# State-space block moved from one software stream to the other, with the loop over batches cut inside the scan

## The chip, the cores and the metric

The kernel runs on one core of a Trainium2 chip. The time is device microseconds from launch to end, the median of several executions. The engines are TensorE (PE), VectorE (DVE), ScalarE (ACT) and GpSimd (POOL); SyncE (SP) only issues DMAs. Each engine works through its own instruction list in order, and waits on semaphores that other engines raise.

## The reference, cut to what matters

Sixteen batches of 512 tokens by 128 channels go through four blocks; batches do not depend on each other.

1. Selective scan, in two directions: after a norm, `delta = softplus(...)`, and for each of 16 states per direction `h[t] = exp(delta*A)[t] * h[t-1] + (delta*B*x)[t]` along the 512 tokens, `y += C*h`. That is 32 scans of 128 x 512 per batch. A feed-forward with a router multiplies the result by a gate.
2. Head of the state-space block: norm, a query projection with rotation, a second norm, and the step sizes `dt` (softplus of 16 numbers per partition, and their running sum `acs`).
3. State-space block in chunks of 128 tokens (`Y_diag` and `Y_off` with decay matrices `exp(segsum)`, a 4-tap convolution, SiLU, a gated norm, output projection).
4. Two transformer layers with local attention (8 heads of 64, windows of 64 tokens), each followed by layer norm and a GELU feed-forward; then the result is multiplied with the state-space result and added to the residual.

```
h = x + o @ wo ;  h = shift_token(h)       # lower 64 channels shifted by one token
```

`shift_token` is why each layer's input lies in a tile `xs0` of 513 columns: channels 0 to 63 at column t, channels 64 to 127 at column t+1.

## The kernel before, in words

A batch's work is written as two streams of numbered slots. Each engine has a generator per part (`prologue`, `scan`, `head`, `stage_b`), and `both` (called from `run`) interleaves them into one instruction list per engine: for each slot of stream B its instructions, then all slots of stream A up to `pace(slot + 1) - 1`. The order is thus fixed by hand through the table `PACE` (pairs of a B slot and an A slot, linear between them).

- Stream A for batch i: `scan(i)`, one slot per state (32), then `A_END` and `head(i)` (8 slots), then `prologue(i+1)` (9 slots: transpose, norm, projections, router feed-forward, `delta`, `u`, the gate).
- Stream B for batch i-1, `stage_b`: 11 slots of the state-space block ("mamba" below), then per layer 15 slots of attention (`UNITS_END`: projections in slots 0 to 3, head-major copies in 2 to 5, eight score units in 4 to 11, their transposes 2 slots and their value products 3 slots later) and 5 slots of output projection, norm and feed-forward; two slots for the final product.

One step of the loop is A of batch i beside B of batch i-1. Before the loop, prologue, scan and head of batch 0 and the prologue of batch 1 run alone (the fill); after it, B of the last batch runs alone (the drain). The last step has no prologue.

A state of the scan takes: PE two selection matmuls `B{k}` and `C{k}` (L505) into PSUM; DVE `bx = u * B` (L1149) from PSUM to SBUF; ACT `dA = exp(...)` (L858) and the copy `Cs` (L864); DVE the scan `hst` (L1157) on `dA` and `bx`; POOL `hc = hst * Cs` (L1392); PE the accumulation of `hc` into bank 2 (L493).

PSUM banks are handed out in rings. Ring A holds banks 0 and 1, ring B banks 3 to 6; banks 2 and 7 are accumulators. A job takes the next bank of its ring and PE waits until the job that had it before was read. `A_JOBS` and `B_JOBS` name each job with the semaphore that tells that it was read. So `B{k}` and `C{k}` alternate between the two banks of ring A, and `B{k}`'s bank is free when `bx` is written:

```
+ [job for k in range(2 * NS) for job in ((f"B{k}", "a_bx", k + 1), (f"C{k}", "a_Cs", k + 1))]
PACE = [(0, 2), (LAYER, 16), (LAYER + UNITS_END, 28), (LAYER + LAYER_SLOTS, HEAD), (LAYER + LAYER_SLOTS + 5, PRO),
        (LAYER + LAYER_SLOTS + UNITS_END, A_SLOTS - 1), (B_END, A_SLOTS - 1), (B_SLOTS, A_SLOTS)]
```

With `LAYER = 11` that puts two states ahead of B's first slot, fourteen more beside the state-space block, twelve beside the attention of layer 0, the head beside the first five slots of layer 1, the prologue beside the rest of its attention, and nothing but the last slot beside the second feed-forward.

The input of a layer is made by one DVE addition over 128 channels (`xa` L1331, `yB` L1351) and two ACT copies of 64 channels each into `xs0` (`shifted`, L784 and L785). ACT holds one set of function tables; `tables()` (L779) loads the set with Exp and Ln, and SiLU or GELU bring a load of their own.

Of the kernel before, what the change touches and what calls it, by code (L numbers as in the profile page):

```python
# [23 lines left out]
P = 128  # L24
# [10 lines left out]
NL = 2  # L35
# [16 lines left out]
def offsets(widths):  # L52
    at, out = 0, {}
    for name, n in widths:
# [16 lines left out]
B_JOBS = ([("ab0", "m_ld", 1)] + [(f"ab{q}", "m_ea", q) for q in range(1, NT)]  # L71
# [3 lines left out]
          + [("y0", "m_y2", 1), ("y1", "m_y2", 2), ("yss", "m_yln", 1), ("mo", "m_sm1", 1)])  # L75
NW = T // WIN
UNITS = [(half, g) for half in range(2) for g in range(HA // 2)]
# [4 lines left out]
for _l in range(NL):  # L82
# [11 lines left out]
    B_JOBS += [(f"wo{_l}", "f_xa", _l + 1), (f"lmean{_l}", "f_xr", _l + 1), (f"lvar{_l}", "f_ln", _l + 1)]  # L94
    for _m in range(3):
        B_JOBS += [(f"fg{_l}{_m}", "f_gl", 3 * _l + _m + 1), (f"fa{_l}{_m}", "f_ha", 3 * _l + _m + 1)]
    B_JOBS += [(f"fd{_l}", "f_y", _l + 1)]


SCAN = 0  # L100
A_END = SCAN + 2 * NS
HEAD = A_END + 1
PRO = HEAD + 8
A_SLOTS = PRO + 9
LAYER = 11
# [4 lines left out]
PACE = [(0, 2), (LAYER, 16), (LAYER + UNITS_END, 28), (LAYER + LAYER_SLOTS, HEAD), (LAYER + LAYER_SLOTS + 5, PRO),  # L110
        (LAYER + LAYER_SLOTS + UNITS_END, A_SLOTS - 1), (B_END, A_SLOTS - 1), (B_SLOTS, A_SLOTS)]


def pace(slot):
    for (b0, a0), (b1, a1) in zip(PACE, PACE[1:]):
        if b0 <= slot <= b1:
# [6 lines left out]
           m_ysq=2, t_xs=2 * NL, f_xs=2 * NL, t_v=7 * NL, t_k=4 * NL, t_r=4 * NL, t_rln=4 * NL, t_clip=4 * NL, t_oT=4 * NL,  # L123
# [4 lines left out]
for _s in ("f_xa", "f_xc", "f_sq", "f_ln", "f_r", "f_xr", "f_hn", "f_y"):  # L128
    PER[_s] = NL


def build(nc, x, wpack, cpack, mask, tables, taps, rowpack, out):
    ctx = ExitStack()
    with ctx:
# [27 lines left out]
        rings = {"A": (banks[0:2], A_JOBS), "B": (banks[3:7], B_JOBS)}  # L162
# [100 lines left out]
        sm = sb("sm", [T])  # L263
        tmp1 = sb("tmp1", [2, T])
# [20 lines left out]
        xsA, x2, xo = xs0, x1b, xa  # L285
        gl, ha = on, kT
        big1 = kT[:, :, :].rearrange("p q (h l) -> p q h l", h=HM)
        big2 = oT[:, :, :].rearrange("p q (h l) -> p q h l", h=HM)
        xbc, sz, y3 = vt[:, 0:4], vt[:, 4:6], PT
        xdt = xdt_b[:, :, :].rearrange("p a (b h d) -> p (a b) h d", b=2, h=HM)  # L290
        xdd = xdd_b[:, :, :].rearrange("p a (b h d) -> p (a b) h d", b=2, h=HM)
        btok = Pm[:, 0, :].rearrange("p (q n) -> p q n", q=NT)
        onf = on[:, :, :].rearrange("p a b -> p (a b)")
# [52 lines left out]
        def run(e, prologue, scan, head, stage_b, finish):  # L346
# [3 lines left out]
            both(chain(scan(2), head(2), prologue(3)), stage_b(1, 0))  # L350
            with e.Fori(3, NB - 1) as i:
                both(chain(scan(i), head(i), prologue(e.snap(i + 1))), stage_b(e.snap(i - 1), e.snap(i - 2)))
            both(chain(scan(NB - 1), head(NB - 1)), stage_b(NB - 2, NB - 3))
            alone(stage_b(NB - 1, NB - 2))
            finish(NB - 1)
# [5 lines left out]
        def _(sp):  # L361
# [17 lines left out]
            def scan(i):  # L379
                yield A_END  # L380

            def head(i):
                yield HEAD

            def stage_b(i, ended):
                yield 2
                if ended is not None:
                    finish(ended)
# [6 lines left out]
            run(sp, prologue, scan, head, stage_b, finish)  # L395
# [4 lines left out]
        def _(pe):  # L400
# [86 lines left out]
            def scan(i):  # L487
# [7 lines left out]

                yield SCAN
                pe.wait_ge(*step("a_parts", i))
                for k in range(2 * NS):
                    yield SCAN + k
# [9 lines left out]
                yield A_END  # L509
                accumulate(2 * NS - 2)  # L510
                accumulate(2 * NS - 1)
# [45 lines left out]
            def stage_b(i, ended):  # L557
                for q in range(NT):
                    yield q // 2
                    if q == 0:  # L560
                        pe.wait_ge(*step("m_acs", i))
                    if used("B", f"ab{q}", i):
                        pe.wait_ge(*vacant("B", f"ab{q}", i))
                    b = bank("B", f"ab{q}")
# [4 lines left out]
                    last.then_inc(full("B", f"ab{q}"), 1)  # L569
                pe.wait_ge(*step("m_h", i))  # L570
                for t in range(4):
                    yield 2 + t
                    if t == 0 and ended is not None:
                        finish(ended)
                    if used("B", f"cx{t}", i):
                        pe.wait_ge(*vacant("B", f"cx{t}", i))
                    b = bank("B", f"cx{t}")
# [3 lines left out]
                    last.then_inc(full("B", f"cx{t}"), 1)  # L581
                for t in range(2):
                    norm_sum("B", f"mz{t}", i, wz_f[:, t * P:(t + 1) * P], hpad[:, 3:3 + T])
                yield 6
                pe.wait_ge(*step("m_xs", i))
                if used("B", "G", i):
                    pe.wait_ge(*vacant("B", "G", i))
                b = bank("B", "G")
                for q in range(NT):
                    ts = slice(q * P, (q + 1) * P)  # L590
                    last = mm(b[:, ts], xbc[:, 2, ts], xbc[:, 3, ts], start=True, stop=True)
                last.then_inc(full("B", "G"), 1)

                for job, t in (("bt", 2), ("xt0", 0), ("xt1", 1)):
                    if job == "xt0":
                        yield 7
                    if used("B", job, i):
                        pe.wait_ge(*vacant("B", job, i))
                    b = bank("B", job)
# [998 lines left out]
```

## Time and profile before

| | |
|---|---|
| median of 3 runs | 4658.02 us (4657.6 to 4661.66) |
| the profiled execution's own time | 4646.64 us |
| its span, first to last instruction | 4644.8 us |
| mean granted TensorE clock | 0.881 of full speed |
| PE busy | 3574.7 us (77% of the span) |
| DVE busy | 2898.1 us (62%) |
| ACT busy | 2356.1 us (51%) |
| POOL busy | 1755.3 us (38%) |
| DMA | mean 4 GB/s over the span |

The sum of all the engines' work is far from filling the span on any one of them, and the shares are averages over stretches with different limits. Matmuls overlap in their pipeline, so PE's busy time is the union of them and not a sum of single durations.

### The profile page before, as it was taken

How to read it: one execution, taken by the hardware profiler on the slowest of the kernel's cores; microseconds unless marked ns; L12 is line 12 of the kernel's file. 1: busy time of each engine (PE TensorE's matmuls, PEld its weight loads, DVE VectorE, ACT ScalarE, POOL GpSimd, SP SyncE). 2: the span in 40 equal slices, each digit the busy share in tenths (PEclk: the TensorE clock that was granted, in tenths of full speed). 3: DMA queues.
4: the chain of work that ended last, by engine and by line, in shares of the span. 5: the costliest groups of instructions: out<-in, count | busy, mean ns of one | idle time of the engine just before them, and what ended most of it. 6: DMA issues, size and time to landing. Idle time of an engine off the chain costs nothing. (4 is left out here: it accounts for less than half of the span.)

```text
span 4644.8 us, 53531 instructions
## 1 busy us (share of the span) xinstructions
PE 3574.7 (77%) x16160; PEld 1947.4 (42%) x16160; DVE 2898.1 (62%) x4687; ACT 2356.1 (51%) x4102; POOL 1755.3 (38%) x1428
## 2 busy tenths in 40 slices
PE   5777777878777777777777787778787877778776
PEld 1244344444444444344443444444344444444443
DVE  6575665757657575665756657566574765757544
ACT  3455555555555555455555555555554554545444
POOL 2253442525325253342534415244252532525332
PEclk9798889989989898888988988899898888979888
DMA  1000000000000000000000000000000000000000
GB/s 74 3 1 1 5 1 5 1 1 5 1 6 1 1 5 1 6 1 6 1 1 6 1 6 1 1 6 1 6 1 1 6 1 6 1 1 3 1 3 3
DMA packets 18378, 20.44 MB, mean 4 GB/s; under 512 B 768, under 2 KB 17152, under 8 KB 17792
## 3 DMA queue, kind: packets, MB, share of 16 engines
q1 hardware_dynamic: 18048, 16.44, 1.1%
q8 instruction: 159, 2.61, 0.2%
q14 instruction: 171, 1.40, 0.1%
HBM read 12.24 MB, written 4.19 MB: 4 GB/s over the span
## 5 line engine op out<-in xcount | busy, mean ns | idle before, releaser
L1392 POOL TENSOR_TENSOR hc<-hst,Cs 128x512 f32<-128x512 f32 x512 | 649.9, 1269 | 1735.9 <-DVE hst L1157 1721.2
L1157 DVE TENSOR_TENSOR_SCAN hst<-dA,bx 128x512 f32<-128x512 f32 x512 | 752.2, 1469 | 313.9 <-issue 164.6
L493 PE MATMUL bank<-hc,C 128*128 128x512 f32 x1024 | 581.8, 652 | 6.9 <-POOL hc L1392 6.9
L517 PE MATMUL bank<-W,xs 128*128 128x512 f32 x960 | 471.4, 628 | 39.0 <-DVE tmp L1298 33.7
L505 PE MATMUL bank<-parts,sel 96*128 96x512 bf16 x1024 | 355.9, 421 | 183.7 <-DVE bx L1149 128.7
L1468 POOL TENSOR_TENSOR Pm<-Pm,rinv 128x512 f32<-128x512 f32 x256 | 273.6, 1069 | 523.3 <-DVE rinv L1314 510.1
L1149 DVE TENSOR_TENSOR bx<-u,bank 128x512 f32<-128x512 f32 x512 | 345.5, 675 | 199.4 <-PE bank L505 170.2
L1453 POOL TENSOR_TENSOR oT<-tmp 128x512 f32<-128x512 f32 x256 | 324.5, 1268 | 273.5 <-DVE tmp L1298 181.8
L864 ACT COPY Cs<-bank 128x512 f32<-128x512 f32 x512 | 294.3, 575 | 244.2 <-PE bank L505 224.1
L983 ACT ACTIVATE Pm<-Pm 128x512 f32<-128x512 f32 x256 | 161.4, 630 | 462.6 <-DVE Pm L1323 462.6
L858 ACT ACTIVATE dA<-delta,neg_a 128x512 f32<-128x512 f32 x512 | 367.9, 719 | 44.1 <-DVE hst L1157 39.2
L683 PEld LDWEIGHTS bank<-kT,qbd 128*128 128x128 f32 x2048 | 313.4, 219 | 50.2 <-issue 37.5
L517 PEld LDWEIGHTS bank<-W,xs 128*128 128x128 f32 x960 | 190.4, 205 | 330.0 <-issue 216.2
L1461 POOL TENSOR_TENSOR oT<-oT,rqk 128x512 f32<-128x512 f32 x256 | 289.9, 1132 | 72.8 <-ACT rqk L961 58.2
L693 PE MATMUL bank<-C,Pm 128*128 128x128 f32 x1024 | 174.7, 297 | 176.9 <-POOL Pm L1468 176.8
L683 PE MATMUL bank<-kT,qbd 128*128 128x128 f32 x2048 | 310.1, 301 | 0.0
L666 PE MATMUL bank<-C,oT 128*128 128x128 f32 x1024 | 179.4, 319 | 116.1 <-DVE tmp L1298 116.0
L751 PE MATMUL bank<-tmp,W 128*128 128x512 f32 (+1 forms) x384 | 213.5, 715 | 69.2 <-DVE tmp L1338 69.2
L493 PEld LDWEIGHTS bank<-hc,C 128*128 128x128 f32 x1024 | 211.4, 210 | 110.1 <-POOL hc L1392 35.2
L505 PEld LDWEIGHTS bank<-parts,sel 96*128 96x128 bf16 x1024 | 91.8, 102 | 393.2 <-DVE bx L1149 199.2
L1293 DVE TENSOR_TENSOR tmp<-bank,rot 128x512 f32<-128x512 f32 x256 | 174.1, 680 | 106.6 <-ACT Pm L952 105.1
L579 PE MATMUL bank<-hpad,wc_f 128*128 128x512 f32 x512 | 229.8, 592 | 0.0
(226 smaller groups left out, 6322.8 us busy)
## 6 DMA issues: line engine op xcount, KB each, us to landing
W<-wpack SPq DMA_DIRECT2D x1, 4498.0 KB, 13.6
x_tok<-x SPq DMA_DIRECT2D x16, 256.0 KB, 2.9
out<-xa SPq DMA_DIRECT2D x16, 256.0 KB, 2.2
rot<-tables SPq DMA_DIRECT2D x2, 512.0 KB, 16.3
wc_f<-taps SPq DMA_DIRECT2D x1, 1024.0 KB, 19.7
C<-cpack SPq DMA_DIRECT2D x1, 721.0 KB, 14.9
Pm<-mask SPq DMA_DIRECT2D x1, 320.0 KB, 15.2
tmp<-rowpack SPq DMA_DIRECT2D x1, 256.0 KB, 17.4
```

The lines of the kernel that those rows point to most:

```text
L493: mm(y_acc[:, :], ident, hc[:, k % 2, :], start=(k == 0), stop=(k == 2 * NS - 1))\
L505: mm(b[:, :], sel16[0:96, o + s:o + s + 1].to_broadcast([96, P]), parts[0:96, d, :], start=True, stop=True)\
L517: mm(b[:, :], weights, rhs, start=True, stop=True).then_inc(full(ring, job), 1)
L683: last = mm(b[:, wi * P:(wi + 1) * P], qbd[:, g, at, :], kT[:, g, lo:lo + P], start=False, stop=(wi == 3), skip_group_check=True)
L858: f(dA[:, k % 2, :], delta[:, k // NS, :], ACT.Exp, scale=neg_a[:, k:k + 1])\
L864: nc.scalar.copy(Cs[:, k % 2, :], b[:, :]).then_inc(sem("a_Cs"), 1)
L1149: v.tensor_tensor(bx[:, k % 2, :], u[:, d, :], b[:, :], ALU.mult).then_inc(sem("a_bx"), 1)
L1157: v.tensor_tensor_scan(o, a, b, 0.0, ALU.mult, ALU.add).then_inc(sem("a_h"), 1)
L1392: g_.tensor_tensor(hc[:, k % 2, :], hst[:, k % 2, :], Cs[:, k % 2, :], ALU.mult)\
L1453: g_.tensor_tensor(qtok[:, 2 * kind + s % 2, :], tmp1[:, kind, :], tmp2[:, kind, :], ALU.add)\
L1461: g_.tensor_tensor(tok, tok, over(rqk[:, s, kind, :], DH), ALU.mult).then_inc(sem("t_qk"), 1)
L1468: g_.tensor_tensor(windows, windows, over(rinv[:, k % 2, :], P), ALU.mult).then_inc(sem("t_P"), 1)
```

## The change

The state-space block becomes a function `mamba` of its own in stream A, between `head` and the next `prologue`. Stream B keeps the two layers and the final product. The loop is cut inside the scan: a step runs the states 12 to 31 of batch i, its head, its state-space block, the prologue of batch i+1 and the states 0 to 11 of batch i+1, beside B of batch i-1.

```
+CUT = 12
 SCAN = 0
-A_END = SCAN + 2 * NS
+A_END = SCAN + 2 * NS - CUT
 HEAD = A_END + 1
-PRO = HEAD + 8
-A_SLOTS = PRO + 9
-LAYER = 11
+MAMBA = HEAD + 8
+PRO = MAMBA + 11
+SCAN1 = PRO + 9
+A_SLOTS = SCAN1 + CUT
+LAYER = 1
-PACE = [(0, 2), (LAYER, 16), (LAYER + UNITS_END, 28), ...
+PACE = [(0, 0), (LAYER, 2), (LAYER + UNITS_END, HEAD + 5), (LAYER + LAYER_SLOTS, MAMBA + 5),
+        (LAYER + LAYER_SLOTS + 7, PRO), (LAYER + LAYER_SLOTS + UNITS_END, SCAN1), (B_SLOTS, A_SLOTS)]
...
+def scan_slot(k):
+    return SCAN1 + k if k < CUT else SCAN + k - CUT
...
+            def ready(i):
+                return chain(prologue(i), scan(i, 0, CUT)) if CUT else prologue(i)
+            def body(i):
+                return chain(scan(i, CUT, 2 * NS), head(i), mamba(i))
-            alone(chain(prologue(0), scan(0), head(0), prologue(1)))
-            both(chain(scan(1), head(1), prologue(2)), stage_b(0, None))
+            alone(chain(ready(0), body(0), ready(1)))
+            both(chain(body(1), ready(2)), stage_b(0, None))
...
+                both(chain(body(i), ready(e.snap(i + 1))), stage_b(e.snap(i - 1), e.snap(i - 2)))
+            both(body(NB - 1), stage_b(NB - 2, NB - 3))
             alone(stage_b(NB - 1, NB - 2))
```

The rings change: bank 3 goes from B to A, so each has three banks. The state-space block's 21 jobs move to ring A, and its tiles now lie in tiles of the scan and the prologue (`hst`, `hc`, `bx`, `gate`, `delta`, `u`, `dA`, `Cs`, `dlow`, `xc`) that are free between a batch's last state and the next prologue. The scan multiplies `B` in place, in PSUM, and reads it there; its bank is free when the scan has ended.

```
-          + [job for k in range(2 * NS) for job in ((f"B{k}", "a_bx", k + 1), (f"C{k}", "a_Cs", k + 1))]
+          + [job for k in range(2 * NS) for job in ((f"B{k}", "a_h", k + 1), (f"C{k}", "a_Cs", k + 1))]
-        rings = {"A": (banks[0:2], A_JOBS), "B": (banks[3:7], B_JOBS)}
+        rings = {"A": (banks[0:2] + banks[3:4], A_JOBS), "B": (banks[4:7], B_JOBS)}
...
-                    v.tensor_tensor(bx[:, k % 2, :], u[:, d, :], b[:, :], ALU.mult).then_inc(sem("a_bx"), 1)
+                    v.tensor_tensor(b[:, :], u[:, d, :], b[:, :], ALU.mult).then_inc(sem("a_bx"), 1)
-                    o, a, b = hst[:, k % 2, :], dA[:, k % 2, :], bx[:, k % 2, :]
+                    o, a, b = hst[:, k % 2, :], dA[:, k % 2, :], b[:, :]
```

DVE now writes the layers' sums straight into `xs0`, in two halves of 64 channels; of ACT's copies into `xs0` only the pair ahead of layer 0 stays. ACT loads the Exp and Ln tables once more, behind the last SiLU of stream B. Inside the block DVE makes the four products with `G` ahead of `xdt`. ACT's copy `x1b` and the output of the batch before move to slots 2 to 4 of layer 0.

```
+HALVES = [(slice(0, 64), 0), (slice(64, P), 1)]
-                    v.tensor_tensor(xa[:, :], xin[:, :], b[:, :], ALU.add).then_inc(sem("f_xa"), 1)
+                    for r, o in HALVES:
+                        v.tensor_tensor(xs0[r, o:o + T], xs0[r, o:o + T], b[r, :], ALU.add).then_inc(sem("f_xs"), 1)
-                    shifted(xsA, xa, "f_xs", "f_xa", i, l + 1)
...
-                    v.scalar_tensor_tensor(out=yB[:, :], in0=b[:, :], scalar=w(f"fb2_{l}"), in1=xa[:, :],
-                                           op0=ALU.add, op1=ALU.add).then_inc(sem("f_y"), 1)
+                    for r, o in HALVES:
+                        dst = xs0[r, o:o + T] if l + 1 < NL else yB[r, :]
+                        v.scalar_tensor_tensor(out=dst, in0=b[r, :], scalar=w(f"fb2_{l}", rows=r), in1=xs0[r, o:o + T],
+                                               op0=ALU.add, op1=ALU.add).then_inc(sem("f_y"), 1)
-                        shifted(xs0, yB, "t_xs", "f_y", i, l + 1)
...
                 f(tmp2[:, 0, :], yB[:, :], ACT.Silu).then_inc(sem("g2"), 1)
+                tables()
...
+                dve.wait_ge(*step("m_G", i))
+                for q in range(NT):
+                    dve.wait_ge(*step("m_L", i, q + 1))
+                    v.tensor_tensor(big2[q], big2[q], each(G[:, q, :], HM), ALU.mult).then_inc(sem("m_M"), 1)
                 for g in range(2):
```

## Rows read from the trace of the kernel before

**Rows 1.** Page, part 1: busy time (share of the span) and instructions of each engine.

```profile
span 4644.8 us, 53531 instructions
...
PE 3574.7 (77%) x16160; PEld 1947.4 (42%) x16160; DVE 2898.1 (62%) x4687; ACT 2356.1 (51%) x4102; POOL 1755.3 (38%) x1428
```

**Rows 2.** Windows, whole steps: stretch, length, PE, PEld, DVE, ACT, POOL busy, clock, DMA.

```profile
208.50:490.50 282.00, 222.17 (x1006) 122.12 (x1006) 179.05 (x292) 146.06 (x256) 110.34 (x89) 0.88 0.00 1
490.50:768.00 277.50, 217.68 (x1010) 121.55 (x1010) 179.96 (x292) 146.34 (x257) 109.42 (x89) 0.91 0.01 3
...
3889.00:4173.50 284.50, 222.81 (x1011) 122.65 (x1011) 179.25 (x291) 145.58 (x255) 110.39 (x89) 0.88 0.01 3
4173.50:4435.80 262.30, 207.05 (x984) 116.30 (x985) 165.02 (x264) 131.00 (x233) 107.13 (x88) 0.88 0.01 2
```

**Rows 3.** Windows, one step: state-space, attention 0, feed-forward 0, attention 1, feed-forward 1.

```profile
2465.50:2528.00 62.50, 53.54 (x219) 29.59 (x220) 44.21 (x60) 31.95 (x52) 27.93 (x21) 0.90 0.03 9
2531.50:2610.00 78.50, 59.88 (x345) 35.07 (x344) 56.66 (x93) 39.63 (x77) 45.86 (x37) 0.91 0.00 1
2610.00:2628.00 18.00, 15.71 (x41) 6.30 (x39) 12.46 (x15) 12.32 (x18) 4.73 (x4) 1.00 0.00 0
2631.00:2726.50 95.50, 72.72 (x372) 43.96 (x370) 53.74 (x111) 46.29 (x87) 30.20 (x26) 0.82 0.00 1
2726.50:2752.00 25.50, 14.60 (x25) 5.14 (x24) 6.92 (x10) 13.29 (x17) 0.00 (x0) 0.78 0.01 3
```

**Rows 4.** Windows, the fill: prologue, scan, end of scan and head, prologue, each alone.

```profile
36.00:70.00 34.00, 25.36 (x53) 9.27 (x53) 14.10 (x28) 18.68 (x26) 2.12 (x1) 0.92 0.03 8
70.00:147.00 77.00, 55.73 (x123) 13.94 (x123) 75.41 (x63) 40.64 (x64) 39.62 (x32) 0.95 0.00 0
147.00:175.50 28.50, 14.91 (x28) 6.39 (x28) 6.69 (x18) 4.99 (x11) 2.20 (x2) 0.55 0.00 0
175.50:208.00 32.50, 24.79 (x50) 9.34 (x49) 14.14 (x27) 18.31 (x26) 2.12 (x1) 0.71 0.03 9
```

**Rows 5.** Windows, the drain: state-space, attention 0, feed-forward 0, attention 1, rest, alone.

```profile
4435.80:4477.50 41.70, 35.19 (x142) 20.56 (x142) 12.91 (x32) 16.29 (x25) 9.11 (x7) 0.84 0.02 7
4477.50:4537.00 59.50, 42.66 (x299) 28.01 (x297) 34.90 (x68) 26.60 (x54) 27.21 (x25) 0.94 0.00 1
4537.00:4560.00 23.00, 15.36 (x28) 5.55 (x28) 4.92 (x7) 9.60 (x13) 0.00 (x0) 0.78 0.00 1
4560.00:4619.00 59.00, 42.41 (x299) 28.11 (x297) 34.91 (x68) 26.59 (x54) 26.80 (x24) 0.94 0.00 1
4619.00:4644.80 25.80, 14.16 (x27) 5.06 (x26) 6.31 (x9) 10.27 (x13) 0.00 (x0) 0.75 0.03 10
```

**Rows 6.** Timeline of DVE in the fill: start, duration, instruction.

```profile
70.11 1.22 DVE L1157 TENSOR_TENSOR_SCAN hst<-dA,bx 128x512 f32<-128x512 f32 x1 [2.49 <-ACT dA L858]
...
71.95 1.82 DVE L1157 TENSOR_TENSOR_SCAN hst<-dA,bx 128x512 f32<-128x512 f32 x1
```

**Rows 7.** The same timeline, POOL.

```profile
71.41 1.27 POOL L1392 TENSOR_TENSOR hc<-hst,Cs 128x512 f32<-128x512 f32 x1 [15.57 <-DVE hst L1157]
```

**Rows 8.** Groups by form, DVE and the copies: instruction, count, busy, mean ns, idle before.

```profile
L1157 DVE TENSOR_TENSOR_SCAN hst<-dA,bx 128x512 f32<-128x512 f32 x512 | 752.2, 1469 | 313.9 <-issue 164.6 <-DVE bx L1149 79.7 <-ACT dA L858 61.7
...
L1345 DVE SCALAR_TENSOR_TENSOR kT<-bank,W,on 85x512 f32<-85x512 f32 x32 | 23.9, 747 | 30.9 <-PE bank L751 30.9
...
L784 ACT COPY xs<-xa 64x512 f32<-64x512 f32 x32 | 19.8, 617 | 124.5 <-DVE xa L1331 124.5
...
L1168 DVE TENSOR_TENSOR x<-xT,xsq 128x512 f32<-128x512 f32 x16 | 11.1, 692 | 0.5
...
L1331 DVE TENSOR_TENSOR xa<-xn,bank 128x512 f32<-128x512 f32 x16 | 11.0, 688 | 41.0 <-PE bank L735 41.0
```

**Rows 9.** One line at a time, scan and `bx`: count, min/median/max ns, first and last start.

```profile
L1157 DVE TENSOR_TENSOR_SCAN hst<-dA,bx x512: 1223/1225/2868, 70.1 to 4332.1; 128x512 f32<-128x512 f32 x171
...
L1149 DVE TENSOR_TENSOR bx<-u,bank x512: 654/677/690, 66.9 to 4330.8; 128x512 f32<-128x512 f32 x171
```

**Rows 10.** The groups by form again, ACT's table loads.

```profile
L779 ACT ACT_TABLE_LOAD x81 | 103.9, 1283 | 25.5 <-DMA rows_b<-rowpack 24.0
```

More of the change, by code:

```diff
@@ L393, in finish @@
                 sp.dma_start(dst, xo[:, :].rearrange("p (q d) -> p q d", q=NT)).then_inc(sem("store"), 16)
-            run(sp, prologue, scan, head, stage_b, finish)
+            run(sp, prologue, scan, head, mamba, stage_b, finish)
             sp.wait_ge(sem("store"), NB * 16)
@@ L494, in accumulate @@
                         .then_inc(sem("a_yacc"), 1)
[L496 to L499, printed above, removed]
+                yield scan_slot(lo)
+                if lo == 0:
+                    pe.wait_ge(*step("a_parts", i))
+                for k in range(lo, hi):
+                    yield scan_slot(k)
                     d, s = k // NS, k % NS
@@ L568, in stage_b @@
                                   start=True, stop=True)
-                    last.then_inc(full("B", f"ab{q}"), 1)
+                    last.then_inc(full("A", f"ab{q}"), 1)
                 pe.wait_ge(*step("m_h", i))
                 for t in range(4):
[L572 to L577, printed above, removed]
+                    yield MAMBA + 2 + t
+                    if used("A", f"cx{t}", i):
+                        pe.wait_ge(*vacant("A", f"cx{t}", i))
+                    b = bank("A", f"cx{t}")
                     for k in range(TAPS):
@@ L718, in stage_b @@
                         n = s - UNIT
+                        if l == 0 and s == 2 and ended is not None:
+                            finish(ended)
                         if s < NT:
@@ L767, in finish @@
                 last.then_inc(sem("xo_full"), 1)
-            run(pe, prologue, scan, head, stage_b, finish)
+            run(pe, prologue, scan, head, mamba, stage_b, finish)
         @block.scalar
@@ L820, in prologue @@
                 yield PRO + 4
+                if later(i):
+                    act.wait_ge(*before("m_sm1", i))
                 for d in range(2):
@@ L849, in prologue, with scan @@
                 tables()
-            def scan(i):
-                yield SCAN
-                act.wait_ge(*step("a_delta", i))
-                for k in range(2 * NS):
-                    yield SCAN + k
+            def scan(i, lo, hi):
+                yield scan_slot(lo)
+                if lo == 0:
+                    act.wait_ge(*step("a_delta", i))
+                for k in range(lo, hi):
+                    yield scan_slot(k)
                     if k >= 2:
@@ L945, in stage_b @@
                         n = s - UNIT
+                        if l == 0 and s == 3:
+                            if ended is not None:
+                                finish(ended)
+                            act.wait_ge(*step("a_x1", i))
+                            nc.scalar.copy(x1b[:, :], x1[:, :]).then_inc(sem("m_x1b"), 1)
                         if s < NT:
@@ L1022, in finish @@
                 nc.scalar.copy(xo[:, :], o_acc[:, :]).then_inc(sem("xo"), 1)
-            run(act, prologue, scan, head, stage_b, finish)
+            run(act, prologue, scan, head, mamba, stage_b, finish)
         @block.vector
@@ L1139, in prologue, with scan @@
                                        op0=ALU.add, op1=ALU.mult).then_inc(sem("a_fo"), 1)
-            def scan(i):
-                yield SCAN
-                dve.wait_ge(*step("a_u", i))
-                for k in range(2 * NS):
-                    yield SCAN + k
+            def scan(i, lo, hi):
+                yield scan_slot(lo)
+                if lo == 0:
+                    dve.wait_ge(*step("a_u", i))
+                for k in range(lo, hi):
+                    yield scan_slot(k)
                     d = k // NS
@@ L1360, in finish @@
                 pass
-            run(dve, prologue, scan, head, stage_b, finish)
+            run(dve, prologue, scan, head, mamba, stage_b, finish)
         @block.gpsimd
@@ L1379, in prologue, with scan @@
                     .then_inc(sem("a_parts"), 1)
-                prior.append(step("a_parts", i))
-            def scan(i):
-                prior.clear()
-                for k in range(2 * NS):
-                    yield SCAN + k
+                pool.wait_ge(*step("a_parts", i))
+            def scan(i, lo, hi):
+                if lo == CUT:
+                    prior.clear()
+                for k in range(lo, hi):
+                    yield scan_slot(k)
                     pool.wait_ge(*step("a_h", i, k + 1))
@@ L1396, in head @@
             def head(i):
-                prior.clear()
                 yield HEAD + 2
@@ L1472, in finish @@
                 pass
-            run(pool, prologue, scan, head, stage_b, finish)
+            run(pool, prologue, scan, head, mamba, stage_b, finish)
 SETUP = 7 + 4 + 3 + 2 + TAPS + 1 + 2 + len(TABLES) * NL
```

309 lines of the change are left out of this document (155 added, 154 removed).

## The prediction, made before the changed kernel was run

> **What bounds the kernel now.** I read the page's busy shares first [rows 1]: PE is busy 77% of the span, DVE 62%, no engine is full, and DMA hardly works. So order and waiting set the time, and the question is in which stretches. The windows of whole steps come next [rows 2]. The span is 208.5 us of fill, fourteen steps from 208.5 to 4173.5 (3965 us, 283.2 each), a last step without prologue of 262.3, and 209 us of drain; the four make 4644.8. The profiled execution took 1.8 us more than its span (4646.6), and the median of the runs is 11.4 above that, so I add 13 to a span to get a median.
>
> One step cut by what stream B does [rows 3] against the same stretches alone in the drain [rows 5] tells what stream A's work costs beside B's:
> - state-space block: 62.5 us and 3.5 more until attention starts at 2531.5, against 41.7; by the pace table 16 states stand up to there, 24.3/16 = 1.5 us each
> - attention 0: 78.5 against 59.5; 12 states, 1.6 us each
> - feed-forward 0: 18 against 23 (the drain's stretch takes in the 3 us of handing over); the last four states cost nothing here
> - attention 1: 95.5 against 59; the head and the prologue cost 36.5 us, and alone they take 28.5 + 32.5 = 61 [rows 4], so 60% of their time shows
> - feed-forward 1: 25.5 against 25.8; nothing hides in it. PE is busy 14.6 of the 25.5 us and DVE 6.9
>
> Stream B alone is 209 us [rows 5], stream A alone 77 + 28.5 + 32.5 = 138 [rows 4]; a step costs B plus 54% of A. The kernel is bound by B's long chain of handovers, on which A's work is laid, with one bare stretch at the step's end. PE's busy share in the stretches is 86, 76, 87, 76 and 57%.
>
> **The change, part by part.**
>
> *Scan in PSUM.* In the fill the first scan takes 1.22 us, the second 1.82 [rows 6], while POOL's `hc` runs until 72.68 [rows 7] and so over its first 0.73 us. The mean of 512 is 752.2/512 = 1.469 us against a median, unhindered, of 1.225 [rows 8, 9]: 125 us of DVE in all, 7.8 per step. With `bx` in PSUM the scan has one input in SBUF. What the trace lacks is a scan with a PSUM input. Bounds: `bx` itself reads PSUM and takes 0.65 to 0.69 us at all 512 places, beside POOL or not [rows 9], against 0.692 for a two-input operation in SBUF alone [rows 8], so a PSUM operand can cost nothing and the scan 1.22 us; or the scan stays at 1.47. I take 1.22, the nearer row being `bx`, that has both POOL's company and a PSUM input. Alone, a state goes from 77/32 = 2.41 us to 0.675 + 1.225 + 0.04 of issue = 1.94. The Trainium skill ("SBUF — State Buffer", Who interferes with whom) says that a VectorE instruction with two SBUF inputs contends with a GpSimd instruction that reads SBUF, and one with at most one SBUF input does not; the first half agrees with the 1.82 us here, and the second would give 1.22. The skill's "VectorE: DVE Perf Modes" (the TRN2 errata) speaks against the edit: it puts a PSUM source at 62 cycles, 65 ns, over an SBUF source, which by an estimate from that page would give 33 us back over 512 scans; the trace does not bear it out (at most 0.69 us for `bx` against 0.692).
>
> *Fill, last step and drain.* Fill: prologue 34 + 36 of loads ahead, 32 states at 1.94 = 62, head 28.5, state-space block 41.7, prologue 32.5, 12 states 23: 258 us, 49 more than now. Drain: 209 - 41.7, less 1 for the copies below = 166. The last step lacks prologue and 12 states: by the prices below (19.5 and 10) 30 us less than a full one.
>
> *The full step.* By the pace table, 20 states stand beside attention 0 (up to its slot 11), the scan's end and five slots of head beside its last slots, the head's rest and the block's slots 0 to 4 beside feed-forward 0, its slots 5 to 10 beside the first seven slots of attention 1, the prologue beside the rest, 12 states beside feed-forward 1. I price each with the shares just found:
> - attention 0: 59.5 + 20 states. They stand twice as dense as now. DVE work is 34.9 [rows 5] + 20 x 1.90 = 73 us, PE 42.7 + 20 x 1.74 (55.7/32 [rows 4]) = 77.5 us less overlap. At 1.5 us each it is 59.5 + 30 = 89.5, 82 to 87% busy on both, as the densest stretches are now. Plus 60% of the head's larger part (21 us): 13. Sum 102
> - feed-forward 0: 23 + 60% of the head's rest (7) and of the block's first half (18): 38
> - attention 1: 59 + 60% of the block's second half (24) and of the prologue (32.5): 93
> - feed-forward 1: 25.5 + 12 states. They alone take 23, B alone 25.5, in turns of 1.7 states a slot; bounds 0 (as the four states in feed-forward 0) and 18 (1.5 each). I take 10: 35.5
>
> That is 268.5 us. Ring B has three banks instead of four: a `q` projection waits for the reader of the `k` before it, not of the `q`. With two states of 1.9 us on DVE between two projection slots PE has the time; I put 0 to 6 us on it, and take 0.
>
> *Halves.* DVE makes two instructions of each of four sums; a form with 85 of 128 partitions takes 747 ns, about what whole sums take (688), so half the partitions save nothing. That is 4 x about 0.72 = 2.9 us more DVE, and six ACT copies of 0.617 less [rows 8]. On B's chain three pairs of copies (1.23 each) turn into one more DVE operation (0.7) each, and the last sum gains one: 0.9 us less, and I take 1.
>
> *Table loads.* Now the gate's SiLU in the prologue's last slot follows B's last SiLU and shares its load and the return. After the change they lie 7 slots apart: two loads more, 2.6 us of ACT per step at 1.283 each [rows 10]. States wait behind the second, B's end before the first: bounds 0 and 2.6, I take 1.5. Also new: GELU with its loads stands in ACT's list between the first states, which the 10 us above hold.
>
> *Waits added.* DVE's `xn2` waits for B's copy of the previous `xn2` (slot 0, long past). ACT's prologue waits for `m_sm1`, five slots back. SP's store moves with B's slot 5 and carries one 256 KB transfer, with a step of room. All at nothing. The selection matmul `C{k+1}` now waits for the end of scan k, and what is queued behind it on PE, B's matmuls, waits too, by up to 1.2 us per pair of states in one slot, eight times in attention 0. DVE has the next scan to do meanwhile. It is in the 1.5 us per state.
>
> Sum per step: 268.5 - 1 + 1.5 = 269. Span: 258 + 14 x 269 + (269 - 30) + 166 = 4429; with the 13, **4442**. In general it is 407 + 15 steps. Each microsecond of the step counts 15 times, so the step decides.
>
> **The rivals.**
>
> *A. Chains of handovers do not hide in each other (slower).* The head's and the block's slots are handovers in series: PE, ACT, PE, ACT, DVE, POOL. So are the feed-forwards'. Beside the projection slots, PE holds at the front of its list a matmul that waits for A's reader (the block's fourth convolution waits for a bank that SiLU, behind B's square and copies on ACT, must free), and B stands. If 80% instead of 60% of head, block and prologue (103 us alone) shows, a step is 269 + 21 = 290 us and the kernel **4757**. It decides from 74%, where the step is 283.4. For it: the head in attention 1 today; PE is only 76% busy there at a clock of 0.82. Against: the state-space block beside states has 86% PE today.
>
> *B. Everything hides (faster still).* Both streams are then about equal, A 62 + 28.5 + 41.7 + 32.5 = 165 and B 166 us alone, and PE's 217 to 222 us per step [rows 2], at 86% busy everywhere, as in the two best stretches, give 255 us: **4232**. For it: balance, and B's bare stretch filled. Against: PE would have to reach this share for a whole step.
>
> *C. The moves cost what they win.* The three-bank ring takes 3 us of its 6, the states beside feed-forward 1 take 15 instead of 10, and the scan stays at 1.47, of which half of the 7.8 us lies on the path: 269 + 3 + 5 + 4 = 281 us and **4622**.
>
> The skill's 65 ns would move the sum by 33 us at most and stays inside the forecast.
>
> **How the numbers follow.** The forecast (a step of 262 to 276 us, 4337 to 4547) gets 0.50, B and what is below 262 0.18, C 0.14 (0.11 clearly faster, 0.03 within 0.2%, about 9 us, which is what can be told from no change), A 0.18. Chances: faster 0.79, same 0.03, slower 0.18. The range reaches from 4280 (a step of 258) to 4690 (285.5), which leaves out a tenth on each side.
>
> **What would show it.** Steps of about 269 us, with PE busy near 81%; scans at 1.22 us, none at 1.8; PE above 80% where B's second feed-forward runs; 258 us to the first full step; six of the explicit table loads a step where there are five (81/16 [rows 10]). I am wrong if the stretch from the scan's end to the prologue (head and block beside feed-forward 0 and the projections) takes over 105 us, for that is where the 60% is least supported, or if scans from PSUM are longer than 1.3 us.

## The result, and the profile after

The changed kernel takes **4887.18 us** (4884.84 to 4897.54, 4 runs) against 4657.81 us before: 1.050 times as long, 95% interval 1.048 to 1.052. 4442 was forecast, and 4280 to 4690 was the range. It is slower where faster was forecast, and slower than the rival A that had the sign (4757).

The page's head of the changed kernel:

```profile
span 4895.7 us, 53911 instructions
...
PE 3675.5 (75%) x16034; PEld 1957.4 (40%) x16160; DVE 2805.9 (57%) x4751; ACT 2365.3 (48%) x4035; POOL 1714.8 (35%) x1428
```

DVE's busy time fell by 92 us (from 2898.1 [rows 1]) and the span grew by 251: DVE stands idle 343 us more. PE's busy time rose by about 100 us (3574.7 before, and 126 of its matmuls have no record here) at a mean granted clock of 0.867 against 0.881. What the lower clock cost by itself no run separates, but it does not order the versions below: e9 has 0.902 and takes 4796 us, e14 has 0.886 and takes 4619. The windows of whole steps, cut where the first state of a step starts, then the last step and the drain:

```profile
256.70:554.40 297.70, 225.21 (x999) 121.82 (x1006) 174.47 (x296) 146.96 (x252) 106.75 (x90) 0.87 0.00 1
...
4171.60:4469.40 297.80, 228.33 (x1003) 121.43 (x1010) 174.33 (x295) 147.33 (x253) 106.11 (x89) 0.87 0.01 3
4469.40:4730.00 260.60, 190.13 (x907) 106.40 (x914) 138.36 (x244) 115.27 (x203) 91.99 (x78) 0.87 0.01 2
4730.00:4895.70 165.70, 116.31 (x650) 67.38 (x654) 82.53 (x156) 74.11 (x132) 53.64 (x48) 0.90 0.01 4
```

The fill is 256.7 us (258 forecast), the drain 165.7 (166). Fourteen steps take 4469.4 - 256.7 = 4212.7 us, 300.9 each, where 269 was forecast and 283.2 stood before [rows 2]. The last step takes 260.6 where 239 was forecast. Of the 467 us by which the span (4895.7) is over its forecast (4429), 446 lie in the fourteen steps and 22 in the last. One step in stretches: from the first rotation of layer 0 (the DVE product of a projection with `rot`, L1328, which is DVE's first work in a layer) to `x1` (the end of the scan's part), to the first rotation of layer 1, to the first state of the next batch, to the next layer 0:

```profile
2366.80:2460.80 94.00, 67.43 (x331) 37.64 (x333) 67.89 (x105) 47.45 (x89) 49.17 (x42) 0.90 0.02 6
2460.80:2516.80 56.00, 44.10 (x147) 21.82 (x148) 16.11 (x43) 17.16 (x30) 2.30 (x2) 0.86 0.00 1
2516.80:2620.80 104.00, 82.06 (x452) 49.16 (x455) 58.94 (x113) 55.85 (x94) 37.21 (x31) 0.87 0.00 1
2620.80:2667.80 47.00, 35.09 (x77) 13.29 (x75) 32.01 (x37) 27.40 (x41) 18.95 (x15) 0.82 0.01 2
```

Against the forecast: 150 for 140 up to layer 1, 104 for 93 beside attention 1, 47 for 35.5 beside feed-forward 1. Each stretch is about 10 us over.

The scan itself did what was forecast. One line (count, min/median/max), then the fill's timeline of DVE and of POOL:

```profile
L1186 DVE TENSOR_TENSOR_SCAN hst<-dA,bank x512: 1220/1221/1222, 69.2 to 4563.3; 128x512 f32<-128x512 f32 x171
```

```profile
71.06 1.22 DVE L1186 TENSOR_TENSOR_SCAN hst<-dA,bank 128x512 f32<-128x512 f32 x1
```

```profile
70.57 1.27 POOL L1429 TENSOR_TENSOR hc<-hst,Cs 128x512 f32<-128x512 f32 x1 [15.24 <-DVE hst L1186]
```

POOL's `hc` overlaps the second scan by 0.78 us, as it did before when that scan took 1.82 [rows 6, 7]. No scan of 512 is longer than 1.222 us.

Two waits stand out. First, PE's wait for the scan (from the waits of the whole kernel: who waited for whom, us, times, longest):

```profile
PE bank L527 <- DVE hst L1186: 388.3, 245, 4.9
```

L527 makes `B{k}` and `C{k}`. In the kernel before the same matmuls waited mostly for the product `bx`, and less:

```profile
PE bank L505 <- DVE bx L1149: 128.7, 58, 4.6
```

One of the new waits, beside feed-forward 1 (timeline):

```profile
2627.04 0.38 PE L527 MATMUL bank<-parts,sel 96*128 96x512 bf16 x1
...
2629.24 1.22 DVE L1186 TENSOR_TENSOR_SCAN hst<-dA,bank 128x512 f32<-128x512 f32 x1
...
2630.52 0.61 PE L527 MATMUL bank<-parts,sel 96*128 96x512 bf16 x1 [3.10 <-DVE hst L1186]
...
2630.92 1.92 PE L514 MATMUL bank<-hc,C 128*128 128x512 f32 x2
...
2632.63 5.78 PE L777 MATMUL bank<-tmp,W 128*128 128x512 f32 x12
```

PE has made `B{k}` at 2627.4 and then stands 3.1 us with `C{k}` in front, whose bank is held until the scan before has ended at 2630.46. The feed-forward's matmuls (L777) stand behind it.

Second, the rotations wait for ACT's squares of the projections (L983): 419.1 us in the changed kernel, 105.1 before (waits of DVE):

```profile
DVE tmp L1328 <- ACT Pm L983: 419.1, 113, 12.8
```

```profile
DVE tmp L1293 <- ACT Pm L952: 105.1, 65, 3.2
```

The longest stand beside attention 1, where DVE waits for ACT, ACT for PE and PE for ACT (timeline of the three):

```profile
2527.78 0.22 ACT L992 ACTIVATE rqk<-rqk 128x16 f32<-128x16 f32 x1
2528.01 1.28 ACT L942 ACT_TABLE_LOAD   x1
...
2530.05 5.93 PE L600 MATMUL bank<-hpad,wc_f 128*128 128x512 f32 x8 [4.60 <-ACT delta L942]
...
2536.01 0.69 ACT L942 ACTIVATE u<-bank,W 128x512 f32<-128x512 f32 x1 [4.87 <-PE bank L600]
```

```profile
2540.27 0.69 DVE L1328 TENSOR_TENSOR tmp<-bank,rot 128x512 f32<-128x512 f32 x1 [12.77 <-ACT Pm L983]
```

The fourth convolution (L600) wants a bank that the first SiLU (L942) frees, and that stands behind ACT's share of the second projection; ACT then waits for this convolution with all of layer 1's squares (L983) behind it, and DVE is idle for 12.8 us.

### The profile page after: what moved, and what is told of

Its sections match the earlier page's. It is cut to its first block, busy times and chain, and to the rows that moved or that the text cites. A ratio compares the mean times of both kernels' runs of the same rounds, so it can differ in the third digit from the quotient of the medians.

```text
span 4895.7 us, 53911 instructions
## 1 busy us (share of the span) xinstructions
PE 3675.5 (75%) x16034; PEld 1957.4 (40%) x16160; DVE 2805.9 (57%) x4751; ACT 2365.3 (48%) x4035; POOL 1714.8 (35%) x1428
## 4 chain that ended last, share of the span: by engine, by line
PE 39%; DVE 31%; issue 14%; ACT 13%; POOL 2%; ACTq 1%; DMA 0%; DVEq 0%; SPq 0%; POOLq 0%
PE bank L540 6%; DVE hst L1186 6%; PE bank L600 5%; PE bank L514 5%; DVE tmp L1333 4%; DVE ssq L1337 3%; DVE Pm L1358 3%; DVE mx L1354 3%; PE bank L777 3%; PE bank L761 3%; PE bank L707 3%; DVE tmp L1328 2%; DVE rsum L1344 2%; PE bank L527 2%; PE bank L690 2%
## 5 line engine op out<-in xcount | busy, mean ns | idle before, releaser
L1186 DVE TENSOR_TENSOR_SCAN hst<-dA,bank 128x512 f32<-128x512 f32 x512 | 625.1, 1221 | 199.2 <-ACT dA L886 76.6
L527 PE MATMUL bank<-parts,sel 96*128 96x512 bf16 x1024 | 398.6, 436 | 413.2 <-DVE hst L1186 388.3
L514 PE MATMUL bank<-hc,C 128*128 128x512 f32 x1024 | 656.4, 728 | 55.6 <-POOL hc L1429 54.3
L1328 DVE TENSOR_TENSOR tmp<-bank,rot 128x512 f32<-128x512 f32 x256 | 175.3, 685 | 419.1 <-ACT Pm L983 419.1
L527 PEld LDWEIGHTS bank<-parts,sel 96*128 96x128 bf16 x1024 | 101.0, 105 | 777.4 <-DVE hst L1186 608.5
L1178 DVE TENSOR_TENSOR bank<-u,bank 128x512 f32<-128x512 f32 x512 | 349.8, 683 | 73.5 <-PE bank L527 72.1
L707 PEld LDWEIGHTS bank<-kT,qbd 128*128 128x128 f32 x2048 | 309.5, 216 | 71.8 <-issue 58.3
L707 PE MATMUL bank<-kT,qbd 128*128 128x128 f32 x2048 | 302.6, 296 | 16.4 <-issue 13.1
L600 PE MATMUL bank<-hpad,wc_f 128*128 128x512 f32 x512 | 261.3, 664 | 68.9 <-ACT delta L942 68.9
L1011 ACT COPY PT<-bank 128x512 f32<-128x512 f32 x256 | 150.0, 586 | 299.0 <-PE bank L717 296.1
L1498 POOL TENSOR_TENSOR oT<-oT,rqk 128x512 f32<-128x512 f32 x256 | 267.1, 1043 | 58.0 <-ACT rqk L992 38.7
L514 PEld LDWEIGHTS bank<-hc,C 128*128 128x128 f32 x1024 | 231.7, 230 | 137.1 <-POOL hc L1429 82.0
L983 ACT ACTIVATE Pm<-bank 128x512 f32<-128x512 f32 x256 | 146.0, 598 | 259.0 <-PE bank L540 258.8
L1354 DVE TENSOR_REDUCE mx<-bank 128x4 f32<-128x512 f32 x256 | 175.3, 685 | 159.5 <-PE bank L707 159.5
```

The source lines that it names most:

```text
L514: mm(y_acc[:, :], ident, hc[:, k % 2, :], start=(k == 0), stop=(k == 2 * NS - 1))\
L527: mm(b[:, :], sel16[0:96, o + s:o + s + 1].to_broadcast([96, P]), parts[0:96, d, :], start=True, stop=True)\
L707: last = mm(b[:, wi * P:(wi + 1) * P], qbd[:, g, at, :], kT[:, g, lo:lo + P], start=False, stop=(wi == 3), skip_group_check=True)
L1178: v.tensor_tensor(b[:, :], u[:, d, :], b[:, :], ALU.mult).then_inc(sem("a_bx"), 1)
L1186: v.tensor_tensor_scan(o, a, b, 0.0, ALU.mult, ALU.add).then_inc(sem("a_h"), 1)
L1354: v.tensor_reduce(mx[:, n % 2, :], windows, AX.X, ALU.max).then_inc(sem("t_max"), 1)
```

## The experiments

Theory 1: PE stands behind `C{k}`. Theory 2: what costs is where the block and its chains of handovers stand, theory P being one reading of it (the block wants PE, as its new neighbours do), theory S another (the cut costs). All are timed in 3 rounds against the kernel before on the same chip; ratios are to that, with 95% intervals. Three chips were used, and the kernel before took 4649 to 4654 us on each, so differences between versions on different chips are good to some 5 us. "Mean of ten" is the mean of ten steps in a version's own trace.

**e1. C{k} first.**

```
-for job in ((f"B{k}", "a_h", k + 1), (f"C{k}", "a_Cs", k + 1))]
+for job in ((f"C{k}", "a_Cs", k + 1), (f"B{k}", "a_h", k + 1))]
-for name, o in (("B", 0), ("C", NS)):
+for name, o in (("C", NS), ("B", 0)):
```

> The changed kernel, but C{k} is asked for ahead of B{k}, so that in the ring of three C{k} waits for the scan before the last and no longer for the last one. Theory 1 (PE stands behind C{k}, which waits for the end of the scan before it: 388 us of such waits in the whole changed kernel): PE's waits for the scan fall from 388 to under 150 us and the kernel from 4887 to 4700 or less. Theory 2 (the moved state-space block and its handovers in series are what costs): the waits fall, and the time stays within 4840 to 4890.

Measured: 4721.4 us, 1.015 (1.013 to 1.018). In its waits the scan is no longer among PE's releasers at the top; part of the wait is now for ACT's copy `Cs`, whose bank the next `B{k}` inherits:

```profile
PE bank L527 <- ACT Cs L892: 184.7, 135, 4.1
PE bank L514 <- POOL hc L1429: 106.0, 116, 3.6
```

The same step in its windows (to layer 1, to the next batch's first state, to the next layer 0):

```profile
2276.10:2421.10 145.00, 112.18 (x483) 59.42 (x482) 83.89 (x147) 64.06 (x119) 50.89 (x44) 0.88 0.02 4
2421.10:2525.10 104.00, 82.56 (x456) 49.11 (x455) 59.20 (x113) 55.48 (x94) 37.15 (x31) 0.87 0.00 1
2525.10:2566.10 41.00, 32.85 (x74) 12.09 (x73) 31.80 (x36) 26.75 (x40) 19.25 (x15) 0.88 0.01 3
```

166 us, 11 per step, went away, 5 and 6 us of it in the two stretches where states stand and none in the one without. Theory 2's interval (4840 to 4890) is missed by far. Theory 1 names a cause, 21 us short of its own figure; 68 us above the kernel before, on the same chip, remain.

**e2. The product in SBUF again**, its bank free at `a_bx`.

```
-  ((f"B{k}", "a_h", k + 1), ...     v.tensor_tensor(b[:, :], u[:, d, :], b[:, :], ALU.mult)
+  ((f"B{k}", "a_bx", k + 1), ...    v.tensor_tensor(bx[:, k % 2, :], u[:, d, :], b[:, :], ALU.mult)
```

> The changed kernel, but the product u*B goes to SBUF again and its bank is free when the product is written; all else, three-bank rings included, as changed. Theory 1: the bank's early release is worth more than the shorter scan: 4700 to 4780 with scans of 1.47 us on the mean. Theory 2: the scan gets 0.25 us longer, 125 us of DVE in all, and nothing else changes: 4900 to 4960.

Measured: 4807.4 us, 1.034 (1.031 to 1.037); its scans take 1.504 us on the mean:

```profile
L1186 DVE TENSOR_TENSOR_SCAN hst<-dA,bx 128x512 f32<-128x512 f32 x512 | 770.2, 1504 | 198.4 <-DVE bx L1178 88.7 <-ACT dA L886 59.1 <-issue 37.5
```

PE now waits for the product, 227.2 us in all, instead of for the scan. 80 us faster than the change: the held bank cost more than the short scan brings. 27 us outside theory 1's interval, and far outside theory 2's.

**e3 and e4. On the kernel before: three-bank rings (with the four products with `G` ahead of `xdt`, as in the change), then the scan in PSUM as well.**

```
-rings = {"A": (banks[0:2], A_JOBS), "B": (banks[3:7], B_JOBS)}
+rings = {"A": (banks[0:2] + banks[3:4], A_JOBS), "B": (banks[4:7], B_JOBS)}
```

> The kernel before, with three banks in each ring instead of two and four, and the four products with G ahead of xdt as the ring then wants; nothing else moved. Theory 1: B's fourth bank is worth something, ring A's third gives some back: 4650 to 4720. Theory 2: the rings are no part of the loss: 4640 to 4670. If it is above 4800, the rings alone explain the result.

> The run with three-bank rings on the kernel before, and the scan in PSUM besides, its bank held until the scan ends. Theory 1: the held bank costs more than the 7.8 us of DVE per step bring: slower than the three-bank run by 50 us or more. Theory 2: it is faster than the three-bank run by some 60 us, half of the 125 us of DVE.

Measured: 4625.1 us, 0.994 (0.991 to 0.996), and 4549.7 us, 0.978 (0.975 to 0.981). The rings with the moved products cost nothing; e3 is even 15 us below both theories' intervals. In the old order the held bank does not undo the short scan: e4 is 75 us below e3, though PE waits 184.5 us for scans there. Theory 1 as a general statement falls: what the wait costs depends on the order around it.

**e5. The block stays in stream B, all else is made** (cut behind 12 states, rings, PSUM, halves, C{k} first). **e6. e4 with C{k} first.**

```
 e5: LAYER = 11;  PACE = [(0, 2), (LAYER, 16), (LAYER + UNITS_END, HEAD + 2), (LAYER + LAYER_SLOTS, HEAD + 6),
        (LAYER + LAYER_SLOTS + 3, PRO), (LAYER + LAYER_SLOTS + UNITS_END, SCAN1), (B_SLOTS, A_SLOTS)]
```

> The state-space block stays in stream B, beside 16 states of the scan; what is left of the change is made: the loop cut behind the first 12 states, three-bank rings, the scan in PSUM, the halves; and C{k} ahead of B{k}. Theory P (the move pairs the block, on which PE works 35 of 42 us, with the projections and the feed-forward, which want PE and whose handovers are in series as its own are, and takes it from the states, which want DVE): steps of 265 to 272 us, the kernel 4400 to 4520. Theory S (the cut itself, twelve states beside the second feed-forward, costs what is lost): no faster than 4600.

> The kernel before with three-bank rings and the scan in PSUM (4549.7 us), and C{k} ahead of B{k}. The same edit took 166 us off the changed kernel. If the wait for the scan before is paid wherever two states follow each other, 4450 to 4500; if only where states stand dense beside attention and feed-forward 1, 4530 to 4555.

Measured: e5 4496.1 us, 0.967 (0.964 to 0.969), in theory P's interval for the time, though its steps (275.5 us, mean of ten) lie above the 265 to 272 that came with it; e6 4511.5 us, 0.971 (0.968 to 0.973), between its two intervals. The cut with the halves and a new table is worth 15 us over e6. C{k} first brings 38 us here against 166 in the change.

**e7. The change with C{k} first, without the cut, and all spread later.**

```
-CUT = 12
+CUT = 0
+PACE = [(0, 0), (LAYER, 2), (LAYER + UNITS_END, 30), (LAYER + LAYER_SLOTS, HEAD + 2),
+        (LAYER + LAYER_SLOTS + 7, MAMBA + 4), (LAYER + LAYER_SLOTS + UNITS_END, PRO), (B_SLOTS, A_SLOTS)]
```

> The changed kernel with C{k} first (4721.4 us), and the cut taken out again: all 32 states at the step's start, the block in stream A, the prologue beside the second feed-forward; the pace table spread to suit. Theory P: the block is still beside the projections of layer 1, and the states are denser beside attention 0: 4700 to 4850. Theory S: faster than 4650.

Measured: 4448.7 us, 0.957 (0.954 to 0.958). Theory P, which had 4700 to 4850, is refuted: with the block in stream A the kernel is faster than e6 and e5. Theory S seemed right, but two things were changed at once, the cut and the table.

**e9. The same without the cut, the pace entries as in the change** (`(LAYER + UNITS_END, HEAD + 5), (LAYER + LAYER_SLOTS, MAMBA + 5)`, `PRO` at +7).

> The changed kernel with C{k} first, CUT = 0, and the pace table's entries as in the changed kernel (head's slot 5 at the end of attention 0, the block's slot 5 at layer 1's start, the prologue over the rest of attention 1), so that only the twelve states move, from beside the second feed-forward to beside attention 0. The other run without the cut (4448.7 us) had the block and the prologue later too. If the cut itself is the loss, 4450 to 4600; if the places of block and prologue are (six SiLUs among the projections), 4680 to 4800.

Measured: 4796.1 us, 1.031 (1.029 to 1.033), at the upper end of the interval of "places". So theory S falls too. With the entries kept, taking the cut out costs 75 us; by the entries alone e7 is 347 us faster than e9. The rotations wait 404 us for ACT's squares in e9 and 115 in e7.

**e8. One entry moved by one slot**, on e1.

```
-(LAYER + LAYER_SLOTS, MAMBA + 5)
+(LAYER + LAYER_SLOTS, MAMBA + 6)
```

> The changed kernel with C{k} first (4721.4 us), and one entry of the pace table moved by one: the block's six SiLUs and its fourth convolution stand ahead of the first projections of layer 1, not between the second and the third. There DVE now waits up to 12.8 us for a square that ACT makes behind the six SiLUs. If that wait is on the path, the step gets 5 to 8 us shorter: 4600 to 4650. If it only moves, 4700 to 4740.

Measured: 4609.4 us, 0.992 (0.989 to 0.994). Its windows, as e1's:

```profile
2224.30:2374.30 150.00, 115.16 (x497) 60.29 (x495) 83.80 (x147) 70.21 (x127) 50.86 (x43) 0.91 0.01 4
2374.30:2462.30 88.00, 71.36 (x441) 43.97 (x440) 57.63 (x112) 49.00 (x86) 37.16 (x31) 0.90 0.00 1
2462.30:2504.30 42.00, 33.85 (x77) 12.31 (x77) 32.64 (x38) 26.85 (x40) 19.37 (x15) 0.88 0.01 3
```

Attention 1 shrank by 16 us, and the stretch before it, where the fourth convolution and the SiLUs now stand, grew by 5. Because the table is linear between its entries, four more of the block's slots move ahead by one, so the 112 us may not be the SiLUs' alone. The rotations' wait for the squares fell with them, by about as much (from 388.2 us in e1):

```profile
DVE tmp L1328 <- ACT Pm L983: 246.0, 110, 9.7
```

The knot of the three engines is a cause, and this entry undoes about half of it.

**e10 and e11. B's first slot ahead of A's leading states, A's last slots ahead of B's last product**, on e7 and on e8.

```
-(LAYER, 2) ... (B_SLOTS, A_SLOTS)]
+(LAYER, 0) ... (B_END, A_SLOTS), (B_SLOTS, A_SLOTS)]
```

The entries at `LAYER + LAYER_SLOTS + UNITS_END` go along, to `PRO + 2` in e10 and `SCAN1 + 1` in e11.

> The run without the cut (4448.7 us) with stream A's last slots emitted ahead of B's last product, and B's first projection ahead of A's first two states of the step. In that run B stands for 18 us from its last product to its next first rotation. If B's chain sets the step, it gets 5 to 10 us shorter: 4300 to 4380; if stream A's does, 4430 to 4460.

> The same two moves on the run with the cut, C{k} first and the SiLUs early (4609.4 us), where B stands for 18 us as well. If B's chain sets the step: 4480 to 4540; if DVE, full with twelve states there, 4590 to 4620.

Measured: e10 4469.7 us, 0.962 (0.958 to 0.965), 21 slower than e7 and 10 above its interval. From B's last product to its next first rotation 4 us pass instead of 18, and the step stays at 271.7 us (means of ten): B's chain at the step's end does not set it. e11 4548.8 us, 0.977 (0.974 to 0.980), 61 faster than e8 and 9 above the interval; there the same shortening brings the step from 282 to 277. Which chain sets the step differs between the two.

**e12. The cut behind 6 states**, entries between e7's and e8's (states to `A_END` over attention 0, `HEAD + 5` at layer 1, `MAMBA + 7` at +7, `PRO + 5` at its end).

> The changed kernel with C{k} first and the loop cut behind 6 states instead of 12, the pace table between those of the run without the cut (4448.7) and of the one with 12 and the SiLUs early (4609.4). If the number of states at the step's end is what costs, about half way, 4500 to 4560; if the cut is neutral and the places of the block matter, near 4450.

Measured: 4453.2 us, 0.957 (0.955 to 0.960), near the 4450 of "neutral". Six states at the end cost nothing that shows against e7's none, in tables that differ too.

**e13 and e14. Twelve states and the block late; e14 is the change itself, B{k} first, with nothing but this table.**

```
+PACE = [(0, 0), (LAYER, 2), (LAYER + UNITS_END, A_END), (LAYER + LAYER_SLOTS, HEAD + 5),
+        (LAYER + LAYER_SLOTS + 7, MAMBA + 7), (LAYER + LAYER_SLOTS + UNITS_END, PRO + 5), (B_SLOTS, A_SLOTS)]
```

> The changed kernel with C{k} first and its 12 states at the step's end kept; by pace alone the states stretch over all of attention 0, the head lies beside feed-forward 0, the block's SiLUs beside attention 1's score units, and the prologue's second half beside feed-forward 1. If the block's place is the cause, as fast as with 6 states: 4440 to 4500. If the number of states at the end costs too, 4520 to 4600.

> The change as it was made, B{k} ahead of C{k}, with nothing but the pace table of the run with the block late. If the wait of C{k} for the scan before costs the same anywhere, 150 to 180 us above that run; if good places hide it, under 80 above.

Measured: e13 4466.2 us, 0.961 (0.959 to 0.963); e14 4618.9 us, 0.993 (0.991 to 0.995). So twelve states cost little as well. The table alone takes 268 us off the change and brings it 0.7% below the kernel before. C{k} first is worth 153 us there, against 166 in e1: the two causes nearly add (434 us apart, 421 together). PE's wait for the scan is even longer in e14 than in the change (404.2 us against 388.3), so the table's gain is not a shorter wait of this kind. The rotations' wait does follow it, first e14's, then e13's:

```profile
DVE tmp L1328 <- ACT Pm L983: 126.6, 81, 4.0
```

```profile
DVE tmp L1328 <- ACT Pm L983: 98.6, 75, 4.0
```

That is near the 105.1 of the kernel before, and 292 us less than in the change, of the same size as the 268 us of time. Two such numbers beside each other do not prove the whole gain to be this wait; e15 below is a case where they part. One step of e14 and one of e13, each to layer 1 and to the next layer 0:

```profile
2237.10:2356.10 119.00, 93.70 (x418) 50.40 (x421) 78.63 (x122) 58.99 (x108) 50.95 (x43) 0.90 0.02 5
2356.10:2524.10 168.00, 133.91 (x587) 73.15 (x590) 97.88 (x174) 88.11 (x147) 56.23 (x46) 0.85 0.01 1
```

```profile
2156.70:2271.70 115.00, 89.67 (x418) 48.48 (x421) 78.41 (x122) 58.25 (x107) 52.05 (x44) 0.92 0.02 5
2271.70:2429.70 158.00, 127.11 (x586) 69.61 (x589) 97.90 (x173) 87.85 (x146) 55.27 (x45) 0.90 0.01 1
```

The first stretch is 31 us shorter in e14 than in the change (150), the rest 17 longer (151). Head and block have moved from the first to the second, and cost less there; which of their slots, these rows do not tell.

**e15. The block alone two to three slots later** (SiLUs behind the last projection), the prologue pressed into seven slots.

> The changed kernel with C{k} first (4721.4 us), and the block alone moved two to three slots later, its SiLUs behind the last projection of layer 1 instead of behind the second; head, states and feed-forward stay, the prologue is pressed into seven slots. If SiLUs among projections are the cause: 4560 to 4640, as with the SiLUs ahead of them (4609.4). If it is head and block beside feed-forward 0, or the whole order, above 4680.

Measured: 4779.0 us, 1.028 (1.026 to 1.030), slower than e1. (The head's last two slots move along, to the end of feed-forward 0.) That SiLUs among projections are the whole of it is refuted: behind them, among the score units and with a hurried prologue, the version is 58 us slower. Its rotations wait less (219.7 us for e1's 388.2), but DVE now waits for score matmuls (L707), 355.1 us against 104.9 in e1:

```profile
DVE mx L1354 <- PE bank L707: 355.1, 66, 11.2
```

The waiting has moved to the score units. In e13 the SiLUs stand among the score units too, two slots later, its prologue is as dense (nine slots beside six of B) but reaches into feed-forward 1, and this wait is 171.5 us; which of the differences does it is open.

**e16. e12 with the moves of e10 and e11 at half strength** (`(LAYER, 1)`, `(B_END, A_SLOTS - 1)`).

> The run with 6 states at the step's end (4453.2 us), one of stream A's two leading states behind B's first slot and A's last states ahead of B's last product. With 12 states these moves brought 61 us, with none they cost 21. If they bring what the states at the end hold up, about 4420 to 4450.

Measured: **4407.9 us**, 0.946 (0.943 to 0.950), 45 us less than e12, 12 below the interval, and the fastest version.

## Why the prediction was wrong

- **What came as forecast**: fill, drain and scan (256.7, 165.7 and 1.221 us against 258, 166 and 1.225), the halves (0.687 and 0.750 us each, for about 0.72) and the table loads (97 of the explicit ones, six a step). What halves and loads cost on the path (-1 and +1.5) no run separates. That the scan in PSUM is worth having was right in the old order (-75 us, e4). In the change e2 shows the opposite, for the next reason.
- **"It is in the 1.5 us per state"**: the wait of `C{k+1}` for scan k was seen, with what stands behind it on PE, and priced at nothing. This is the first step that failed. It costs 11 us per step (e1), 153 to 166 us in all. The argument was that DVE has the next scan to do meanwhile. But PE stands until 0.06 us after the scan before, and B's matmuls behind it begin that much later, 3.1 us in the rows above and 4.9 at the longest, where at most 1.2 was assumed. With this wait alone away (e1) the kernel is still 68 us slower than before.
- **"I price each with the shares just found"**: this is the second, and the larger. The 60% came from a head and a prologue over the 15 slots of attention 1, and was put on a block that had never stood there, and on stretches that it was not read from. Beside attention 1 the block and the prologue came to 104 for 93, up to layer 1 it was 150 for 140. Rival A's knot of fourth convolution, SiLU and squares is there, and e8 takes 7.5 us per step by one entry, the late table (e14) 18. In e13, without the wait for the scan and with little of the knot, the two stretches together take 233 us (mean of ten), which is the forecast's 140 + 93, though its order is another. So a sum by this share can come out, in an order whose chains do not lock into each other; that the share is right for each part no run shows. The order that locks them was named as a rival and given 0.18.
- **Twelve states beside feed-forward 1**, 10 us taken, bounds 0 and 18: measured 47 - 25.5 = 21.5 us, outside the bounds, of which 6 are the wait for the scan (15.5 in e1). DVE is 32 us busy of e1's 41 there, and 17 to 18 us pass from stream B's last product to its next first rotation in the change and in e1, 4 in e11 (means of ten).
- **What remains of 32 us per step**: 11 by e1, 7.5 by e8, 4 by e11, whose own steps are 277 us on the mean of ten. That leaves 8 us over the forecast, and e13 goes 4 us below e11 by its table. Which slot pairs do it stays open, and e15 shows that one guess at it was wrong.
- **Rival A** had the sign and a step of 290 of 300.9. Its reading, that 80% instead of 60% shows, describes only this table: with the same instructions in another order e14's step is 283 and e13's 272 (means of ten), and it holds nothing of the wait for the scan.
- **The signs.** The one that was to show the prediction wrong did: from the scan's end to the prologue 124 us pass (mean of ten), more than 105. But the fast versions are over it too (e13 113, e7 115), so it does not tell a good order from a bad one. PE is busy 76% of a step for the 81% expected, and 75% beside feed-forward 1. The 13 us from span to median did not hold either: the median is 8.5 us below the profiled span, which was the slowest of the four executions.

## What to carry to other kernels

A share read from one neighbourhood does not price a move into another: before pricing, follow the new instruction lists around the moved block and look for a wait behind which stands what another engine needs in order to end it. In a ring of PSUM banks, name for each job the last reader of the bank that it inherits; holding a bank longer was cheap here once the job that inherits it was not the next one wanted (swapping two jobs: 166 us). When one change moves work and sets a new hand-made order, try the order by itself before judging the move: here the table alone spans 4619 to 4887 us for the same work.

## What the runs showed of the hardware

- A scan with one input in PSUM takes 1.221 us at all 512 places (1.220 to 1.222), also where a product of GpSimd overlaps it by 0.78 us, and with both inputs in SBUF 1.504 us on the mean of the same program (e2). The Trainium skill ("SBUF — State Buffer", Who interferes with whom) states that a VectorE instruction with at most one SBUF input does not contend with GpSimd, and the runs agree.
- Writing a product to PSUM instead of SBUF costs 7 ns: `u*B` takes 0.684 us at the median written to PSUM, 0.677 written to SBUF [rows 9].
- e7 loads tables 30 times ahead of the prologue's GELU, the change 16 times. The 14 loads more, 1.283 us each, are 18 us of ACT, and e7 is still among the fastest; what they cost on its path no run separates.
